# Order of one vector-engine beat in the routing stage, and constant multiplications on TensorE in the trace back of a decoder layer

## The reference

```python
x = x + state_space_scan(layernorm(x))         # 16 states for each of 256 channels, over 256 steps
x = x + align(ctx, layernorm(x))               # dynamic time warping, below
x = x + experts(layernorm(x))                  # 64 experts, each token goes to its 2 best

# align, for each of the 16 batch items: D = distances 256 x 256, R = accumulated cost,
# walk back from the far corner to the origin:
choice = argmin([R[i-1, j-1], R[i-1, j], R[i, j-1]])
expanded = zeros(256, 256).at[j_idx].add(ctx[i_idx] * valid)

# experts:
weights, selected = top_k(x @ gate, 2); weights = softmax(weights)
sort tokens by expert;  out = (silu(x @ w0[e]) * (x @ w1[e])) @ wo[e]
```

## Time and profile before

| what | us |
|---|---|
| median of 3 runs | 1336.68 (1336.24 to 1340.41) |
| the profiled execution's own time | 1337.79 |
| its span | 1335.9 |
| `trace_back`, from its first instruction to the last copy | 665.6 to 739.6 |
| `expand` | 739.9 to about 861 |
| `experts` | about 861 to 1297 |
| `combine`, to the end | 1297.4 to 1335.9 |

### The profile page before, as it was taken

How to read it: one execution, slowest core, us unless ns; L and a number is a source line. 1 busy time by engine, 2 the same in 40 slices (tenths; PEclk the granted TensorE clock), 3 DMA queues, 4 the chain that set the end, 5 groups by cost and what they waited for, 6 DMA issues and landing times. The chain is left out here.

```text
span 1335.9 us, 20510 instructions
## 1 busy us (share of the span) xinstructions
PE 999.3 (75%) x6641; PEld 904.7 (68%) x6641; DVE 894.0 (67%) x2026; ACT 580.0 (43%) x1287; POOL 659.4 (49%) x602
## 2 busy tenths in 40 slices
PE   3568777787878867577640786399999999999940
PEld 2557667676767767466520575299999999999930
DVE  2899999999999998488798687133333333333318
ACT  3667786868687765344340464022122222222200
POOL 5987868687787872200000177443444454454410
PEclk9998999989999999655585898599999999999985
DMA  7544464655656561112203011398888888999729
GB/s 222 178 120 155 153 172 158 164 165 138 186 146 173 161 185 48 44 32 44 52 34 126 32 52 45 108 325 254 273 282 278 286 287 293 309 292 314 266 69 341
DMA packets 163530, 232.60 MB, mean 174 GB/s; under 512 B 34380, under 2 KB 87996, under 8 KB 162656
## 3 DMA queue, kind: packets, MB, share of 16 engines
q1 hardware_dynamic: 145808, 207.79, 50.8%
q0 software_dynamic: 11280, 19.06, 4.3%
q10 hardware_dynamic: 6336, 4.44, 1.0%
HBM read 203.08 MB, written 23.95 MB: 170 GB/s over the span
## 5 line engine op out<-in xcount | busy, mean ns | idle before, releaser
L942 PE MATMUL st_y_ps<-ident,st_hc 128*128 128x128 f32 x2048 | 273.8, 291 | 111.9 <-DVE st_hc L527 111.9
L942 PEld LDWEIGHTS st_y_ps<-ident,st_hc 128*128 128x128 f32 x2048 | 255.8, 203 | 134.2 <-DVE st_hc L527 133.4
L410 POOL TENSOR_TENSOR st_u<-st_dx,codes 128x1024 f32<-128x1024 f32 x128 | 298.8, 2355 | 43.0 <-DVE st_h L519 42.5
L519 DVE TENSOR_TENSOR_SCAN st_h<-st_da,st_u 128x512 f32<-128x512 f32 x256 | 298.5, 1210 | 9.6 <-POOL st_u L410 9.6
L2125 PE MATMUL mo_h<-mo_xt,w 128*128 128x128 f32 (+17 forms) x2048 | 279.9, 288 | 1.9 <-DVE mo_xt L2222 1.9
L2125 PEld LDWEIGHTS mo_h<-mo_xt,w 128*128 128x128 f32 x2048 | 269.5, 192 | 6.3 <-issue 2.5
L2228 DVE TENSOR_TENSOR mo_inter<-mo_silu,mo_h 128x128 f32<-128x128 f32 (+17 forms) x256 | 77.9, 304 | 248.3 <-ACT mo_silu L2199 244.0
L684 ACT ACTIVATE st_da<-st_delta,st_a_neg 128x510 f32<-128x510 f32 x256 | 171.6, 685 | 66.4 <-DVE st_h L519 59.3
L2199 ACT ACTIVATE mo_silu<-mo_h 128x128 f32<-128x128 f32 (+17 forms) x256 | 74.2, 290 | 284.5 <-PE mo_h L2125 284.5
L2066 POOL DMA_INDIRECT outs<-mo_o,choice x95 | 93.4, 983 | 206.3 <-DVE mo_o L2239 193.1
L527 DVE TENSOR_TENSOR st_hc<-st_h,st_cps 128x1024 f32<-128x1024 f32 x128 | 153.6, 1201 | 0.0
(11 more groups left out here) (340 smaller groups left out, 1370.2 us busy)
## 6 DMA issues: line engine op xcount, KB each, us to landing
codes<-bc SPq DMA_DIRECT2D x256, 256.0 KB, 3.7
w<-in_L_ffn_w_dram SPq DMA_DIRECT2D x128, 512.0 KB, 5.4
wo<-in_L_ffn_wo_dram SPq DMA_DIRECT2D x64, 512.0 KB, 7.3
co_got<-outs SPq DMA_DIRECT2D x16, 512.0 KB, 5.9
wave<-dist SPq DMA_DIRECT2D x16, 274.0 KB
x<-in_x_dram SPq DMA_DIRECT2D x8, 512.0 KB, 8.7
st_cx<-in_ctx_dram SPq DMA_DIRECT2D x8, 512.0 KB, 4.0
dist<-st_dd SPq DMA_DIRECT2D x32, 128.0 KB, 3.0
```

Source lines behind the costliest of these rows:

```text
L410: nc.gpsimd.tensor_tensor(u_sb[k % URING][:, :, :], dx[p % 2][:, :, :], over_chunks(b_sb[k % BRING]), ALU.mult).then_inc(u_ok, 1)
L519: nc.vector.tensor_tensor_scan(h_sb[k % HRING][:, dh, :], da_ps[dh][:, :], u_sb[k % URING][:, dh, :], 0.0, ALU.mult, ALU.add).then_inc(h_o ...
L942: m = nc.tensor.matmul(y_ps[t // 2][:, t % 2, dh * P:(dh + 1) * P], hc_sb[k % RING][:, dh, t * P:(t + 1) * P], K.ident[:, :], start=False, ...
```

## The change

Three edits:
1. In `trace_back`, TensorE makes 58 products of two constants (`K.one16` by `K.below`, fp16, 128 x 512) while VectorE makes the lookups: two products each time that `st` shows another lookup to begin, for the first 29 of 32. They go to `ex_ps[0]`, which nobody reads any more.
2. In `expand`, TensorE makes six such products into `l_ps[1]` before the first `expanded(0)`. They wait for nothing.
3. In VectorE's beat, `pick`, `position` and `address` of item b-3 stand right behind `statistics(b)`, ahead of `largest(b-2)`; before, they stood between the later steps. `aggregate` and `nearness` stand between them, and `invert` and `newton(b, 0)` follow `largest` and `where`.

```diff
@@ trace_back @@
         MAPPED = 2 * BR
+        LOOKING = MAPPED + BLK + 1
@@ trace_back, vector @@
             did(nc.vector.tensor_scalar(twice[:, :], entry[:, :], 2.0, None, ALU.mult))
+            assert n[0] == LOOKING
@@ trace_back, tensor @@
                 nc.tensor.matmul(s_ps[:, 0:1], shift[:, :], found[:, :], start=True, stop=True).then_inc(shifted, 1)
+            for i in range(BR - 3):
+                pe.wait_ge(st, LOOKING + 2 * i)
+                for j in range(2):
+                    nc.tensor.matmul(ex_ps[0][:, :], K.one16[:, :], K.below[:, :, :].rearrange("p i l -> p (i l)"),
+                                     start=True, stop=True)
             pe.wait_ge(gathered, BLK)
@@ expand, vector @@
                 if real(b):
                     statistics(b)
+                if real(b - 3):
+                    pick(b - 3)
+                if real(b):
+                    aggregate(b)
+                if real(b - 3):
+                    position(b - 3)
+                if real(b):
+                    nearness(b)
+                if real(b - 3):
+                    address(b - 3)
                 if real(b - 2):
                     largest(b - 2)
                 if real(b):
-                    aggregate(b)
+                    invert(b)
                 if real(b - 2):
                     where(b - 2)
                 if real(b):
-                    nearness(b)
-                if real(b - 3):
-                    pick(b - 3)
-                if real(b):
-                    invert(b)
+                    newton(b, 0)
                 if real(b - 2):
                     mark(b - 2)
-                if real(b):
-                    newton(b, 0)
-                if real(b - 3):
-                    position(b - 3)
                 if real(b):
                     newton(b, 1)
                 if real(b - 2):
                     choose(b - 2)
                 if real(b):
                     newton(b, 2)
-                if real(b - 3):
-                    address(b - 3)
-                if real(b):
                     newton(b, 3)
@@ expand, tensor @@
+            for i in range(6):
+                nc.tensor.matmul(bank(l_ps[1]), K.one16[:, :], K.below[:, :, :].rearrange("p i l -> p (i l)"),
+                                 start=True, stop=True)
             expanded(0)
```

## The result

Ratio of the changed kernel to the one before: 0.9973, 95% interval 0.9966 to 0.998, from 20 executions of each.

A forecast was written before the change was run, and what follows sets the result against it. It took GpSimd's fixed row of bucket writes, started by the first slots, to bound the end of `expand`. Order 1.9 and six products 1.25 from the median 1336.68 gave 1333.5 us, the 58 products 0; range 1330.5 to 1336.6.

The forecast's parts named there:

- What bounds the kernel: In `expand`, the experts' start hangs on the first slots, then GpSimd's fixed 80 us of bucket writes, then their landing.
- Order: In VectorE's beat, `address` 1.75 to 1.9 us behind `statistics`, first slots 2.15 us earlier; 1.9 after the landing's cost.
- The price in the steady beat: In VectorE's beat, the moved steps fill 0.90 us of idle time ahead of `largest`, so they cost 0.
- Tail: In the last three beats of `expand`, 0.5 to 0.9 us each, some 1.9 earlier for `ORDER` and SP's first weights.
- The landing: At the end of `expand`, the last bucket write meets the end of the weights: cost 0.25 us, bounds 0 to 0.6.
- Six products: At the start of `expand`, the clock rises sooner: 1.7 us gained from the profiled execution, 1.25 from the median.
- 58 products: Beside the lookups in `trace_back`: cost 0 and most likely gain 0, the clock being down again when `expand` begins.
- The rival in which it holds: Clock stays up into `expand` or rises early, landing costs nothing: 1331.9 us, down to 1331.3; chance 0.20.
- The total: Whole kernel: 1333.5 us from the median of 1336.68; 3.6 us less than the profiled execution's 1337.79, so 1334.2.
- VectorE as bound: In the beat of `expand`, VectorE grows slower than GpSimd's 5.10 us; a 5.55 us beat would give 1340.7; chance 0.04.
- the change does not do all it says: Products only delay `expanded(0)` by 0.3, or the write lands behind the weights: 1335.1 us, up to 1336.7; chance 0.22.

The follow-up runs named there:

- order in the tail alone: VectorE's new order in the last three beats (16 to 18) only, no constant products, against the kernel before: 1336.99 us, one execution.
- change without the 58: The whole change less the 58 products beside the lookups, against the kernel before: 1334.26 us, ratio 0.9974.
- six alone: Only the six constant products ahead of `expanded(0)`, added to the kernel before: 1336.62 us, ratio 0.9997; repeated on a slower chip: 0.9996.
- order alone: Only VectorE's new order, in all beats, applied to the kernel before: 1336.14 us, ratio 0.9994; repeated on a slower chip: 1.0001.
- 58 alone: Only the 58 constant products beside the lookups, added to the kernel before: 1337.16 us, ratio 0.9999; its profiled execution took 1333.61.
- order in beat 3: VectorE's new order in beat 3 only, the first with slots, no constant products, against the kernel before: 1337.67 us, one execution.
- clock held: The change plus products beside all 32 lookups, between VectorE's small steps and behind the transposes, against the kernel before: 1333.92 us, ratio 0.9969.

## Why the prediction was right, step by step

The step that carries it, GpSimd's row behind the first slots, was right. That the totals lie as close as 3.2 and 2.94 is partly luck, as the later points show.

- **What bounds the kernel: right.** GpSimd's row has a fixed length (80.30 to 80.41 us from first write to last in the eight kernels of the table that have one order in all beats), and what came earlier in front of it came earlier behind it: 1.75 + 2.35 = 4.10 in front, 4.14 at the experts. With the order in the tail alone the row was 80.76, for a reason that I did not find.
- **Order: 2.15 predicted for the slots, 2.35 measured**, 1.57 behind `statistics` in place of 1.75 to 1.9. The sum was wrong in itself: its terms (0.75, 0.41, 0.2, 0.41, some 0.15 for `nearness`, and twice 0.1) make 2.1, not 1.75 to 1.9, and would have given 1.8 at the slots. The mis-sized term is the listed durations taken as if they followed end to end: neighbours overlap by 0.37 in all, and the two waits of 0.1 do not show. That 2.15 came near 2.35 is luck of that slip. At the experts it was 2.06 (alone) and 2.55 (change without the 58 against six alone). The price in the steady beat was 0, as predicted.
- **Tail: no effect, and its size right in part by luck.** SP's first weights moved 2.24 us against `added(0)`, predicted 1.9. With order alone they moved 1.64: TensorE's three waits there are 1.93, 1.08 and 1.94 us in place of 2.59, 1.48 and 2.33, so 0.4 to 0.7 each and not 0.5 to 0.9. In the change the clock fell a little later (822.5) against the beats, and one `logits` took 1.12 us in place of 1.91. The run with the order in the last three beats only moved them 0.8, since the first of the three waits is for a step of the beat before, and shows that this buys nothing.
- **The landing: the step was wrong, its term small.** I had the last write of before land into free engines, since the DMA share had dropped by 845.4, and priced its meeting with the weights at 0.25. In fact the kernel before landed no faster than the change, and without weights in flight the change landed in 2.05. Both events moved together (6.30 and 6.29 us apart), so nothing changed: -0.17 where +0.25 was forecast, and 3.41 where the wait was to be 3.6 to 4.2. A low DMA share in the microsecond of a write does not say that the write is undisturbed.
- **Six products: 1.7 in the profiled execution, measured 1.75**; `added(0)` at 5.75 into the block, the rise 3.4 us into it (middle of the forecast 3.8). As the typical value I took 1.25. The profiles without the six have 7.50, 7.47, 7.62, 7.81 and 6.62, mean 7.40; those with the six at the change's clock 5.75, 5.84, 5.65 and 6.29, mean 5.88: 1.5, so 1.25 was somewhat low.
- **58 products: 0 predicted, 0 measured** (0.9999 alone; 0.9973 with, 0.9974 without). The clock was down again at 737.1. The rival in which it holds was wrong for the change (and its lower end was added up wrongly: 2.15 and 2.8 from 1336.68 give 1331.7, not 1331.3), but its mechanism is real: with the gaps filled it held, for 0.84 us more, not the 1.35 that the rival's 2.6 had over 1.25, because VectorE's `ex_on` is late next.
- **The total: 3.2 predicted, 2.94 measured**, in spite of 4.1 at the experts' start. From the profiled execution I had forecast 3.6 there, so 0.5 too little (the landing 0.4, the slots 0.2), and misses in the other direction cancel it. The prediction took it that what reaches the experts reaches the end, and had no term for what they do with it. Their stage is 436.0 us in the profiles of before and of the 58 alone, and 437.4 to 438.9 in the eight others of that speed, also in the three in which the stage before is as long as in before (six alone, order in beat 3 or in the tail only). So it is not the earlier start that is taken back. All eight have the stretch at the lower clock near 1277; before and the 58 alone do not. The rest of the spread is the clock at the stage's start: it rises 4.8 to 7.6 us behind the experts' first product. Taking 436.0 for the 5.0 us of before, 0.5 us more for each further microsecond at the lower clock, and 1.47 for the late stretch, gives all ten stages within 0.2 us (order alone: 7.0 us, 438.5 against 438.65; clock held: 7.6, 438.8 against 438.92). So what the experts gave back is TensorE's clock, at the start and near 1277, and none of their work. Why it rises and falls when it does there is open, and so is whether the change has a part in it. With one profile of before at this speed I can't say whether 436.0 is its rule or its luck: the other short stage is in the fastest of eleven executions. The profile of before on the slower chip could not tell, as its experts took 475.7.
- **Do the parts add up?** By trace yes: 2.06 for order and 1.66 for six alone make 3.7; both together 4.4, and 4.1 in the change. By time order alone gave 1.16 and six alone 0.68, together 1.8, and the two in one kernel 3.04. The intervals reach 2.0 and 1.6 us for the single ones, so this is no contradiction, and it is not shown to be agreement either.
- **The rivals**: VectorE as bound was refuted (`logits` 4.92 us apart, and GpSimd waits for slots once, 17.3 us ahead of its first write); "the change does not do all it says" was refuted by 5.75 and 13.59, though its 1335.1 lies only 0.5 from what was measured.

## What to carry to other kernels

When one engine has a row of work of fixed length and the work behind hangs on its end, find what starts the row: two microseconds there came from nothing but an order of instructions, in idle time that was already paid, though the order had to hold beyond the first beat. In this kernel 58 products of constants with one gap of 4.1 us behind them gave nothing that could be measured, and six right in front of the work brought its first result 1.5 us forward. Take one part out of a change before keeping it all: the kernel without its first edit is as fast and simpler. And before crediting a difference between two profiles to an edit, look at the granted clock in the stages that it does not touch: here it moved the experts by up to 3 us.

## What the runs showed of the hardware

- In TensorE's idle time ahead of the transposes, 4.11 us in both, the clock fell 3.0 us after the last product in the change (734.15, 737.12) and 4.6 us after it with the 58 alone (731.50, 736.11), there behind the start of the transposes. In the kernels without the six products it rose 3.0 us (58 alone) to 5.5 us (order in beat 3 only) after TensorE's first product of `expand`, 4.7 in before; `added(0)` came 6.62 to 7.81 us into the block. So both delays differ between executions of the same code at that place.
- The clock's rise behind the experts' first product came 4.8 to 7.6 us after it, and the stage was 0.5 us longer for each further microsecond.
- A 128-row indirect write issued behind 512 KB loads took 2.84 to 3.87 us from the end of its issue to the waiting gather, and 2.05 with none of these loads in flight (one profile).
- Small VectorE instructions (758.3 to 760.0 in the change) begin 0.04 to 0.09 us before the listed end of the one ahead when they do not read its result; `position` and `address`, which read a result, begin 0.07 and 0.04 behind the listed end of the one that made it. Sum start to start, not durations.
- On two other chips the same program took 4.5 and 4.7% longer; on the second, DMA ran at 267 GB/s through the experts (900 to 1250 us) in place of 287, and TensorE was busy 332.5 of 350 us in place of 350. Which of the two causes the other is not shown. What binds a stage on one chip need not bind it on another.
